# Second attention's score maxima as 32-row tiles in four banks, without head-separated keys

## The chip, the cores and the metric

The kernel runs on one core of a Trainium2 chip. The metric is the device time of one execution in microseconds (us). The engines are named as the profile names them: PE (TensorE matmuls), PEld (TensorE weight loads), DVE (VectorE), ACT (ScalarE), POOL (GpSimd) and SP (SyncE, which issues DMAs). PSUM, which the matmuls write, has eight banks of 512 float32 per partition.

## The reference

Two batches of 512 tokens with 128 features pass four sublayers, each after a layer norm and each added to its input: attention over a context of 154 keys (8 heads of 64), a feed-forward layer with 16 routed experts, attention over the same context (16 heads of 8), and a feed-forward layer with 8 routed experts.

```python
x = x + _L0_xattn_ref(_layernorm(x), ctx_768, ...)
x = x + _L0_ffn_ref(_layernorm(x), ...)
x = x + _L1_xattn_ref(_layernorm(x), ctx_768, ...)
x = x + _L1_ffn_ref(_layernorm(x), ...)
# the second attention, 16 heads of 8 features
scores = jnp.einsum('bhqd,bhkd->bhqk', q, k) * scale
weights = jax.nn.softmax(scores, axis=-1)
out = jnp.einsum('bhqk,bhkd->bhqd', weights, v)
```

## The kernel before

The work is cut into named steps: `h1` is one 128-wide hidden tile of a feed-forward layer for one batch, `down` the product back to 128 features, `score` and `pT` belong to the first attention. A table of strings, `PROGRAM`, writes out for each engine the order in which it takes its steps, and for PE also the PSUM bank behind each step (`score1.2` writes bank 2). Engines meet through two counters per bank: `wait_filled` waits until PE has filled a bank, `wait_moved` and `wait_bank_free` wait until a reader has emptied it. PE takes its steps strictly in the table's order, so a step whose bank is not free holds up all behind it.

The second attention of a batch b works on four groups g of four heads. In the features of a group, head j owns rows 32j to 32j+31 (its 8 features in several rounded parts, and two rows that carry the maximum). Its steps are, in order:

- `qd`, `q1` (PE, L1375): queries of all groups, four 32-row tiles at a time, one per group, copied to SBUF by ACT (`q1copy`, L828).
- `k1` (once for the kernel): the keys of a group, assembled by ACT (`rounded`) and DVE in `k_stack`. From this, `place_k1` on ACT (L817, 16 instructions) writes a tile `k1` in which each head's keys stand alone, with zeros in the other heads' rows, and `place_k1s` on POOL writes a like tile for the last 26 keys.
- `score1` (PE, L1384, 64 matmuls): scores for the maxima alone. All 128 rows of one group's queries for 128 tokens (t) are the stationary operand, and the head-separated keys of two heads, 308 columns, stream through. One matmul fills one bank.
- the same step on DVE (L1143, 64 reductions): the negated maxima of 2 heads by 128 tokens.
- `mT` (L1392): transposes the maxima of half h (two groups); ACT copies them and a DMA (`place_max`) writes them into rows of `q1`, after which `expT` (L1404) and `expR` (L1411) compute scores less maxima, transposed. ACT takes the exponentials (L845, L852).
- `rest1` and `pv1` (L1424, L1435), `od`, `oT`, `onT`, `wo1`: weighted values, division by the sums, output projection. Then the layer norm (`lnA`, `lnB`, `xT`), the router (`gate`, `route`), and the last feed-forward layer.

The lines of the step that changes:

```python
# PE, L1379 to L1385
b, t, g, half = step[1:]
wait_moved(pe, ("q1", b, g))
pe.wait_ge(k1_placed, 4 * (g + 1))
filled(pe.matmul(bank(step)[:, 0:2 * CTX]..., q1[:, b, g, t * P:(t + 1) * P],
                 k1[:, b, g, 2 * half:2 * half + 2, 0:CTX], start=True, stop=True), step)
# DVE, L1139 to L1145
wait_filled(dve, step)
moved(dve.tensor_reduce(neg_max1[:, b, g // 2, 2 * half:2 * half + 2, g % 2, t],
                        bank(step)[:, 0:2 * CTX]..., AX, ALU.max, negate=True), step)
```

Of the kernel before, what the change touches and what calls it, by code (L numbers as in the profile page):

```python
# [54 lines left out]
P = 128  # L55
B = 2
# [24 lines left out]
REST_SETS = ((0, 1), (2, 3))  # L81
LAST = (3, B - 1, N_HID[3] - 1)
# [4 lines left out]
def all_steps():  # L87
# [39 lines left out]
    steps += [("place_k1", g, j) for g in groups for j in range(4)]  # L127
# [49 lines left out]
    "ACT":  # L177
        "kT split lnB kT xT kT kT lnB q xT q split " + 16 * "score " +
        "pT score score pT k1 pT score pT score score split score pv pv score pv pv place_k1 score score " +
        "score score score split score score place_k1 pT score score place_k1 lnB pT k1 pT xT split k1 pT " +  # L180
# [24 lines left out]
        "hsplit h3 hsplit hsplit h3 res res res res last_res last_res ",  # L205
    "Pool":
        "lnA split lnA bo bo split " + 7 * "norm " + "lnA norm place_k1s split split split lnA place_k1s " +
        8 * "weigh " + "split split lnA " + 8 * "weigh " +
        "split split lnA split place_k1s place_k1s split split split lnA split split weigh weigh weigh weigh " +
        "weigh lnA " + 27 * "weigh ",  # L210
    "SP":
# [1327 lines left out]
```

## Time and profile before

| | |
|---|---|
| median of 3 runs (lowest to highest) | 231.21 us (231.13 to 231.42) |
| span of the profiled execution, first to last instruction | 229.8 us |
| median less that span | 1.4 us |
| PE busy | 223.2 us (97%), 1389 instructions |
| DVE / ACT / POOL busy | 163.5 / 155.3 / 126.4 us |
| TensorE clock granted | 1.00 of full speed in the whole span |

A busy time counts an instruction from its start to a modelled end, and matmuls overlap in the pipeline, so PE busy at 97% doesn't say that PE works at its best pace. The pace is read from starts: how long after one piece's first instruction the next piece's first instruction begins. A float32 matmul has two records in the trace, a matmul of rounded operands (fp32r) one. The profile gives no time of its own for the profiled execution besides the span; the 1.4 us between the span and the median are taken as lying around it.

### The profile page before, as it was taken

Reading aid. Unit: us, or ns where it says so; the run is one execution under the profiler, and the core shown is the slowest. Engines: PE = TensorE matmul, PEld = TensorE weight load, DVE = VectorE, ACT = ScalarE, POOL = GpSimd, SP = SyncE. Lnnn points to the kernel's source line nnn. Section 1 sums busy time; section 2 is a strip of 40 time slices with the busy share of each in tenths; the row PEclk is TensorE's granted clock in tenths of the full one; section 3 lists DMA queues with packets and bytes.
Section 4 is the critical chain, followed back from the end, with each engine's and each line's share of the span. In section 5 each row is a group of like instructions: output and inputs, shape, how many; then the busy total and the mean of one; then the engine's idle time right before and its main releaser. Section 6 shows DMA issues by size and latency. Waiting matters only on the chain.

```text
span 229.8 us, 4648 instructions
## 1 busy us (share of the span) xinstructions
PE 223.2 (97%) x1389; PEld 166.4 (72%) x1389; DVE 163.5 (71%) x480; ACT 155.3 (68%) x378; POOL 126.4 (55%) x127
## 2 busy tenths in 40 slices
PE   7999999999999999999999999999999999999994
PEld 3576765974989898889535563588878887888873
DVE  3689984788667953699948983564857776776874
ACT  2589999986678446662689788876365686645561
POOL 2766742898057927856592107209499400996540
PEclk9999999999999999999999999999999999999999
DMA  6890000000038924800600000037000003600002
GB/s 208 198 303 8 0 3 0 0 3 1 3 93 230 365 105 165 203 0 4 219 3 0 7 0 6 0 82 287 3 0 0 1 3 105 265 0 4 1 0 91
DMA packets 10174, 17.07 MB, mean 74 GB/s; under 512 B 3715, under 2 KB 5540, under 8 KB 9766
## 3 DMA queue, kind: packets, MB, share of 16 engines
q1 hardware_dynamic: 9926, 16.45, 23.1%
q10 hardware_dynamic: 224, 0.32, 0.4%
q8 instruction: 12, 0.20, 0.4%
q14 instruction: 12, 0.10, 0.1%
HBM read 16.08 MB, written 0.62 MB: 73 GB/s over the span
## 4 chain that ended last, share of the span: by engine, by line
PE 83%; ACT 6%; DVE 3%; DMA 2%; SPq 2%; POOL 2%; issue 1%; DVEq 0%; POOLq 0%
PE psum L1170 12%; PE psum L1173 11%; PE psum L1171 11%; PE psum L1326 7%; ACT prob L748 5%; PE psum L1384 5%; PE psum L1333 4%; PE psum L1335 3%; PE psum L1334 3%; PE psum L1435 3%; PE psum L1278 3%; PE psum L1288 3%; PE psum L1404 2%; PE psum L1256 2%; PE psum L1245 2%; DMA ctxT<-in_ctxT 2%
## 5 line engine op out<-in xcount | busy, mean ns | idle before, releaser
L702 POOL TENSOR_TENSOR act_s<-act_s,spread 128x512 f32<-128x512 f32 x35 | 44.4, 1292 | 19.8 <-DMA spread<-cw 13.6
L1170 PE MATMUL psum<-xT_hi,w_hi 128*128 128x512 f32 x108 | 43.9, 406 | 0.0
L1173 PE MATMUL psum<-xT_lo,w_hi 128*128 128x512 f32 x108 | 42.2, 391 | 0.0
L1171 PE MATMUL psum<-xT_hi,w_lo 128*128 128x512 f32 x108 | 42.2, 391 | 0.0
L797 ACT CAST q<-psum 128x512 fp32r<-128x512 f32 x35 | 20.4, 586 | 20.3 <-PE psum L1335 13.7
L1006 DVE TENSOR_TENSOR q<-psum,q 128x512 fp32r<-128x512 f32 x35 | 23.8, 687 | 13.3 <-ACT q L797 13.0
L787 ACT ACTIVATE act_s<-psum 128x512 f32<-128x512 f32 x39 | 23.0, 597 | 12.3 <-PE psum L1173 7.9
L1143 DVE TENSOR_REDUCE neg_max<-psum 128x2 f32<-128x308 f32 x64 | 26.2, 471 | 4.9 <-PE psum L1384 4.7
L702 POOL TENSOR_TENSOR hid<-hid,spread 128x512 f32<-128x512 f32 x13 | 16.6, 1297 | 18.9 <-DMA spread<-cw 14.6
L652 POOL TENSOR_TENSOR rstd<-vareps,minus_half 128x4 f32<-128x4 f32 x8 | 8.1, 1014 | 33.9 <-DVE vareps L907 33.9
L646 POOL TENSOR_TENSOR w_lo<-w_src,w_hi 128x768 fp32r<-128x768 f32 x12 | 21.7, 1830 | 8.9 <-ACT w_hi L717 8.9
L748 ACT ACTIVATE prob<-psum,neg_max 128x154 f32<-128x154 f32 x64 | 24.0, 405 | 1.7 <-DVE neg_max L949 1.0
L1170 PEld LDWEIGHTS psum<-xT_hi,w_hi 128*128 128x128 f32 x108 | 20.3, 188 | 5.5 <-ACT od L860 0.8
L1173 PEld LDWEIGHTS psum<-xT_lo,w_hi 128*128 128x128 f32 x108 | 20.3, 188 | 4.5
L676 POOL TENSOR_TENSOR prob_n<-prob,row_inv 128x1024 f32<-128x1024 f32 x8 | 15.2, 1899 | 13.9 <-DVE row_inv L956 13.9
L1171 PEld LDWEIGHTS psum<-xT_hi,w_lo 128*128 128x128 f32 x108 | 20.4, 188 | 3.3
L845 ACT ACTIVATE probT<-psum 128x512 f32<-128x512 f32 x32 | 16.8, 604 | 3.5 <-PE psum L1404 3.4
L1326 PEld LDWEIGHTS psum<-w,hid 128*128 128x128 f32 x144 | 17.5, 191 | 1.0 <-issue 0.4
L1326 PE MATMUL psum<-w,hid 128*128 128x128 f32 x144 | 18.1, 275 | 0.0
L1384 PE MATMUL psum<-k,q 128*128 128x308 f32 x64 | 16.0, 342 | 0.6 <-DVE neg_max L1143 0.5
L949 DVE TENSOR_REDUCE neg_max<-psum 128x2 f32<-128x308 f32 x32 | 13.5, 463 | 4.2 <-PE psum L1245 4.0
L1384 PEld LDWEIGHTS psum<-k,q 128*128 128x128 f32 x64 | 10.3, 188 | 8.1 <-DVE neg_max L1143 4.6
(171 smaller groups left out, 468.2 us busy)
## 6 DMA issues: line engine op xcount, KB each, us to landing
spread<-cw SPq DMA_DIRECT2D x16, 256.0 KB, 4.4
spread<-cw SPq DMA_DIRECT2D x6, 512.0 KB, 5.5
w_src<-in_w SPq DMA_DIRECT2D x2, 1152.0 KB, 5.3
w_src<-in_w SPq DMA_DIRECT2D x1, 2304.0 KB, 12.4
spread<-cw SPq DMA_DIRECT2D x8, 128.0 KB, 2.9
w<-in_w SPq DMA_DIRECT2D x1, 576.0 KB, 6.9
out<-X SPq DMA_DIRECT2D x4, 128.0 KB, 1.8
wv<-in_wv SPq DMA_DIRECT2D x2, 192.0 KB, 4.8
```

What stands on the lines that cost most here:

```text
L646: pool.tensor_tensor(lo, src, hi.bitcast(F32), ALU.subtract).then_inc(lo_of[name], 1)
L702: pool.tensor_tensor(g, g, spread[:, slot, :], ALU.mult).then_inc(weighed, 1)
L748: ins = act.activation(prob[:, r, h, 0:CTX], bank(step)[:, m * CTX:(m + 1) * CTX], ACT.Exp, bias=neg_max0[:, b, t, h:h + 1], accum_out=row ...
L787: moved(act.activation(act_buf(n), bank(step), ACT.Silu), step)
L797: act.copy(hid_hi[:, m % 2, :], bank(("h3",) + step[1:])).then_inc(hid_rounded, 1)
L1006: moved(dve.tensor_tensor(hid_lo[:, m % 2, :], bank(h3), hid_hi[:, m % 2, :].bitcast(F32), ALU.subtract), h3)
L1143: moved(dve.tensor_reduce(neg_max1[:, b, g // 2, 2 * half:2 * half + 2, g % 2, t], bank(step)[:, 0:2 * CTX].rearrange("p (j c) -> p j c", ...
L1170: pe.matmul(dst, w_hi, xT_hi[:, b, :], start=True, stop=False)
L1171: pe.matmul(dst, w_lo, xT_hi[:, b, :], start=False, stop=False)
L1173: return pe.matmul(dst, w_hi, xT_lo[:, b, :], start=False, stop=True)
L1326: ins = pe.matmul(bank(key)[:, t * P:(t + 1) * P], hid[:, n % HIDS, t * P:(t + 1) * P], w2_0[:, i, :], start=(i == 0 and t == 0), stop=las ...
L1384: filled(pe.matmul(bank(step)[:, 0:2 * CTX].rearrange("p (j c) -> p j c", j=2), q1[:, b, g, t * P:(t + 1) * P], k1[:, b, g, 2 * half:2 * h ...
```

## The change

- The four heads of a group are read in place. `k1` becomes the tile that DVE assembles (`k_stack` is gone), 16 `place_k1` instructions on ACT and the semaphore `k1_placed` go, and with them DVE's and PE's waits on it.
- `score1` becomes 12 steps (batch, half h, part c) in place of 64. A step covers three, three or two of the eight pairs (g, t) of a half (`PEAKS`). For each pair it issues four matmuls, one per head j, with 32 rows of queries as the stationary operand and 154 key columns, at the four row positions of the array, each into its own bank. So a step has 12 or 8 matmuls, takes four banks, waits for all four to be free before its first matmul, and signals each with its last. In all 128 matmuls stand for 64.
- `peak` is the reduction on DVE: one per bank, 3 x 154 = 462 elements (32 of them) or 308 (16), 48 in place of 64.
- `expT` reads the same keys from the new tile. All orders in `PROGRAM` are written anew, for every engine.

```diff
+PEAKS = ((0, 3), (3, 6), (6, 8))
...
-    steps += [("place_k1", g, j) for g in groups for j in range(4)]
-    steps += [("score1", b, t, g, half) for b in batches for h in range(2) for t in range(T) for g in REST_SETS[h] for half in range(2)]
+    steps += [("score1", b, h, c) for b in batches for h in range(2) for c in range(len(PEAKS))]
+    steps += [("peak", b, h, c, j) for b in batches for h in range(2) for c in range(len(PEAKS)) for j in range(4)]
...
-        "q1.1.6.0.4 pv1 score1.1 score1.7 expR.6 score1.2 expR.0 score1.1 score1.4 score1.7 expT.6.2 score1.1 " +
+        "score1.7.2.1.5 expR.4 expR.6 expT.7.4 pv1 expT.2.6 score1.1.5.7.4 rest1 pv1 score1.2.6.1.5 expT.7.4 " +
...
-                k1 = sb("k1", [P, B, G1, 4, CTX], F32R, r2)
+                k1 = sb("k1", [P, G1, B, CP], F32R, r2)
-                    k_stack = sb("k_stack", [P, 2, B * CP], F32R, r3)
...
-                    act.mul(k1[:, :, g, j, :], k[:, :, 0:CTX], head_rows[:, j:j + 1]).then_inc(k1_placed, 1)
...
+                    key = ("score1",) + step[1:]
+                    wait_filled(dve, key)
+                    moved(dve.tensor_reduce(neg_max1[:, b, h, j, lo:hi],
+                                            bank(key)[:, 0:(hi - lo) * CTX].rearrange("p (i c) -> p i c", i=hi - lo), AX, ALU.max,
+                                            negate=True), key)
...
+                    b, h, c = step[1:]
+                    keys = [step + (j,) for j in range(4)]
+                    for key in keys:
+                        wait_bank_free(pe, key)
+                    lo, hi = PEAKS[c]
+                    for n in range(lo, hi):
+                        g, t = REST_SETS[h][n // T], n % T
+                        wait_moved(pe, ("q1", b, g))
+                        wait_moved(pe, ("k1", g))
+                        for j, key in enumerate(keys):
+                            rows = slice(PAD * j, PAD * j + PAD)
+                            ins = pe.matmul(bank(key)[:, (n - lo) * CTX:(n - lo + 1) * CTX], q1[rows, b, g, t * P:(t + 1) * P],
+                                            k1[rows, g, b, 0:CTX], start=True, stop=True, skip_group_check=True,
+                                            tile_position=(PAD * j, 0))
+                            if n == hi - 1:
+                                filled(ins, key)
```

The second batch's part of the second attention on PE, from its queries (`q1`) on, stood so before; `q,k` of 128x308 is `score1`, `q,k` of 128x512 is `expT`, `probT,v` is `pv1`, `rest_exp,vs` is `rest1`:

```order
L1375 MATMUL psum<-qd,sel 128x512 x8
L1435 MATMUL psum<-probT,v 32x512 x4
L1384 MATMUL psum<-k,q 128x308 x2
L1411 MATMUL psum<-q,k1s 128x512
L1384 MATMUL psum<-k,q 128x308
L1411 MATMUL psum<-q,k1s 128x512
L1384 MATMUL psum<-k,q 128x308 x3
L1404 MATMUL psum<-q,k 128x512 x2
L1384 MATMUL psum<-k,q 128x308
L1404 MATMUL psum<-q,k 128x512 x2
L1384 MATMUL psum<-k,q 128x308 x3
L1424 MATMUL psum<-rest_exp,vs 32x512 x8
```

and stands so now, with `score1` at L1377 (128x154), `expT` at L1399, `expR` at L1406, `pv1` at L1430, `rest1` at L1419:

```order
L1360 MATMUL psum<-qd,sel 128x512 x8
L1430 MATMUL psum<-probT,v 32x512 x4
L1377 MATMUL psum<-k,q 128x154 x12
L1406 MATMUL psum<-q,k1s 128x512 x2
L1399 MATMUL psum<-q,k 128x512 x2
L1430 MATMUL psum<-probT,v 32x512 x4
L1399 MATMUL psum<-q,k 128x512 x2
L1377 MATMUL psum<-k,q 128x154 x12
L1419 MATMUL psum<-rest_exp,vs 32x512 x8
L1430 MATMUL psum<-probT,v 32x512 x4
L1377 MATMUL psum<-k,q 128x154 x8
L1399 MATMUL psum<-q,k 128x512 x2
```

Single score matmuls strewn between other steps have become blocks of 12 or 8. In `PROGRAM` the first three blocks take the banks 7 2 1 5, then 1 5 7 4, then 2 6 1 5; the two `expT` between the first and the second block take 7 4 and 2 6.

At the start of the program, PE stood so before; `wv,ctxT` of 128x512 is `vf`, the values of one batch for the first attention, 128x256 is `vf1`, `ident,xn` is `xT`:

```order
L1186 MATMUL psum<-ctxT,wk 128x320 x4
L1226 MATMUL psum<-ident,xn 128x128 x4
L1202 MATMUL psum<-wv,ctxT 128x512
L1202 MATMUL psum<-wv,ctxT 128x256
L1170 MATMUL psum<-xT_hi,wq_hi 128x512
```

and stands so now:

```order
L1171 MATMUL psum<-ctxT,wk 128x320 x4
L1187 MATMUL psum<-wv,ctxT 128x512
L1211 MATMUL psum<-ident,xn 128x128 x4
L1187 MATMUL psum<-wv,ctxT 128x512
L1187 MATMUL psum<-wv,ctxT 128x256
L1155 MATMUL psum<-xT_hi,wq_hi 128x512
```

The second batch's `vf` now comes before the first query product; before, it stood behind the seventh `scores` step. At the end of the first attention two hidden tiles of the next layer (`h3.2 h1.0`) now stand ahead of the last `pT` steps, where before they came after the values.

## Rows read from the trace of the kernel before

**Rows 1.** The page's head: span, busy time and instructions of each engine.

```profile
span 229.8 us, 4648 instructions
PE 223.2 (97%) x1389; PEld 166.4 (72%) x1389; DVE 163.5 (71%) x480; ACT 155.3 (68%) x378; POOL 126.4 (55%) x127
```

**Rows 2.** Busy time by stretch: us, PE, PEld, DVE, ACT, POOL, clock, DMA share, GB/s.

```profile
13.80:52.90 39.10, 38.09 (x353) 28.61 (x352) 31.93 (x81) 35.49 (x154) 24.70 (x24) 1.00 0.09 25
...
109.30:120.30 11.00, 10.41 (x70) 4.61 (x69) 7.68 (x24) 8.18 (x17) 8.26 (x11) 1.00 0.35 116
120.30:136.30 16.00, 15.81 (x104) 9.50 (x100) 14.45 (x40) 12.93 (x25) 2.47 (x2) 1.00 0.01 3
...
150.00:224.00 74.00, 74.00 (x340) 60.70 (x339) 51.78 (x112) 45.01 (x82) 42.49 (x36) 1.00 0.17 58
```

**Rows 3.** Timeline of PE, 16 to 51 us: start, busy us, what [idle before, releaser].

```profile
16.80 0.79 PE L1245 MATMUL psum<-k,q 64*128 64x154 f32 x8 [0.38 <-ACT prob L748]
17.54 1.12 PE L1202 MATMUL psum<-wv,ctxT 96*128 96x512 f32 x2
18.28 0.62 PE L1170 MATMUL psum<-xT_hi,wq_hi 128*128 128x512 f32 x1
...
50.92 1.28 PE L1256 MATMUL psum<-ident,prob_n 128*128 128x128 f32 x10 [0.53 <-POOL prob_n L679]
```

**Rows 4.** Timelines of ACT and DVE, 8 to 11 us: the first query product's operands.

```profile
8.76 0.58 ACT L728 CAST xT_hi<-psum 128x512 fp32r<-128x512 f32 x1 [0.27 <-PE psum L1226]
...
9.94 0.68 DVE L912 TENSOR_TENSOR xT_lo<-psum,xT_hi 128x512 fp32r<-128x512 f32 x1
```

**Rows 5.** Timeline of PE, 95 to 99 us, and PEld's row of the first step.

```profile
95.57 0.30 PEld L1375 LDWEIGHTS psum<-qd,sel 32*128 32x128 f32 x8
...
95.57 0.74 PE L1375 MATMUL psum<-qd,sel 32*128 32x512 f32 x8
96.24 1.16 PE L1326 MATMUL psum<-w,hid 128*128 128x128 f32 x8
...
98.22 0.87 PE L1384 MATMUL psum<-k,q 128*128 128x308 f32 x5
98.92 0.39 PE L1170 MATMUL psum<-xT_hi,w_hi 128*128 128x512 f32 x1
```

**Rows 6.** Timeline of PE: one and three `scores` steps of the first attention.

```profile
22.43 0.79 PE L1245 MATMUL psum<-k,q 64*128 64x154 f32 x8
23.16 0.66 PE L1256 MATMUL psum<-ident,prob_n 128*128 128x128 f32 x4
...
37.41 1.84 PE L1245 MATMUL psum<-k,q 64*128 64x154 f32 x24
```

**Rows 7.** Timeline of PE, 109 to 110 us: `expT`, then `score1`.

```profile
109.31 0.49 PE L1404 MATMUL psum<-q,k 32*128 32x512 f32 x2
109.74 0.55 PE L1384 MATMUL psum<-k,q 128*128 128x308 f32 x2
```

**Rows 8.** Timeline of PE, 52 us: two of the router's sixteen narrow matmuls.

```profile
52.18 0.26 PE L1300 MATMUL psum<-gates_parts,xT_hi 128*128 128x32 f32 x1
52.29 0.26 PE L1301 MATMUL psum<-gates_parts,xT_lo 128*128 128x32 f32 x1
```

**Rows 9.** Timeline of DVE: reductions, and two products of 512 elements.

```profile
105.59 1.27 DVE L1108 TENSOR_TENSOR hid<-psum,act_s 128x512 f32<-128x512 f32 x2
...
120.72 2.79 DVE L1143 TENSOR_REDUCE neg_max<-psum 128x2 f32<-128x308 f32 x7 [2.46 <-PE psum L1384]
...
135.65 0.48 DVE L1143 TENSOR_REDUCE neg_max<-psum 128x2 f32<-128x308 f32 x1 [0.23 <-PE psum L1384]
```

**Rows 10.** Timeline of ACT, 119 to 122 us; and `place_k1` among the groups by line.

```profile
119.35 2.05 ACT L828 CAST q<-psum 128x512 fp32r<-128x512 f32 x4 [0.66 <-PE psum L1375]
121.26 1.13 ACT L852 ACTIVATE rest_exp<-psum 128x512 f32<-128x512 f32 x2
...
L817 ACT ACTIVATE k<-k_stack,head_rows 128x308 fp32r<-128x308 f32 x16 | 8.1, 547 | 0.0
```

More of the change, by code:

```diff
@@ L206 @@
-    "Pool":
[L207 to L210, printed above, removed]
[20 rows of a table added]
+    "ACT":
+        "split kT kT lnB kT xT lnB split kT q q xT score score score score score score score score score score " +
+        "score score score score score score pT score score score score pT pT score pT k1 score split pv score " +
+        "pv pv pv score score split score score score score pT score score score lnB pT k1 xT pT h1 pT gate k1 " +
+        "k1 pv pv split pv pv h1 cwT h1 h1 h1 lnB xT gate h1 h1 split h1 h1 h1 cwT h1 h1 h1 h1 lnB split xT qd " +
+        "h1 h1 split q1copy q1copy q1copy q1copy split h1 split h1 split mT exp exp exp exp expR exp lnB expR xT " +
+        "exp exp qd mT exp q1copy q1copy q1copy q1copy expR expR exp exp exp exp od exp exp exp exp mT od split " +
+        "expR exp exp onT expR exp mT exp exp exp exp exp expR lnB expR xT exp exp exp exp exp exp exp route exp " +
+        "h1 cwT split h1 hsplit od h1 h1 od h1 hsplit h1 h1 hsplit onT hsplit h1 hsplit h1 split hsplit hsplit " +
+        "h1 h1 hsplit h1 h1 hsplit h1 hsplit lnB hsplit split h1 xT hsplit h1 hsplit hsplit h1 route hsplit h1 " +
+        "h1 hsplit h1 h1 cwT hsplit h1 h1 h1 h1 hsplit hsplit hsplit ycopy hsplit h1 h1 hsplit hsplit hsplit h1 " +
+        "h1 hsplit ycopy hsplit h1 h1 h1 hsplit h1 h1 hsplit hsplit h1 hsplit hsplit hsplit hsplit h1 hsplit " +
+        "hsplit ycopy ycopy ",
@@ L211 @@
     "SP":
-        "store spread spread spread spread spread fetch store spread spread spread spread spread place_max " +
-        "fetch place_max place_max place_max store spread spread spread spread spread store spread spread " +
-        "spread spread spread out out out out ",
+        "store spread spread spread spread spread fetch store spread spread spread spread spread place_max fetch " +
+        "place_max place_max place_max store spread spread spread spread spread store spread spread spread " +
@@ L215 @@
+        "spread spread out out out out ",
 }
@@ L221, in takes @@
     if engine == "PE":
-        return True
-    if kind in ("scores", "q1", "expT"):
+        return kind != "peak"
+    if kind in ("scores", "q1", "expT", "score1"):
         return False
@@ L260, in bank_uses @@
             keys = [step[:3] + (2 * step[3] + j,) for j in range(2)]
+        elif kind == "score1":
+            keys = [step + (j,) for j in range(4)]
         elif kind == "pv1":
@@ L421, in build @@
         k1_rounded = sem("k1_rounded")
-        k1_placed = sem("k1_placed")
         sel_built = sem("sel_built")
@@ L810, in _ @@
                     act.copy(rounded[:, g % 2, 0:B * CP], bank(step)[:, 0:B * CP]).then_inc(k1_rounded, 1)
-                elif kind == "place_k1":
-                    g, j = step[1:]
-                    wait_moved(act, ("k1", g))
-                    act.wait_ge(loaded["const"], 16 * N_CONST)
-                    k = k_stack[:, g % 2, :].bitcast(F32).rearrange("p (b c) -> p b c", b=B)
-                    act.mul(k1[:, :, g, j, :], k[:, :, 0:CTX], head_rows[:, j:j + 1]).then_inc(k1_placed, 1)
                 elif kind == "qd":
@@ L857, in _ @@
                         wait_filled(act, ("oT", 0, k))
-                    act.wait_ge(k1_placed, 4 * G1)
-                    act.wait_ge(k1s_placed, G1)
+                    wait_moved(act, ("k1", G1 - 1))
                     moved(act.copy(od[:, k, :], bank(("pv1", b, k))), ("pv1", b, k))
@@ L1115, in _ @@
                     dve.wait_ge(loaded["const"], 16 * N_CONST)
-                    if g >= 2:
-                        dve.wait_ge(k1_placed, 4 * (g - 1))
-                        dve.wait_ge(k1s_placed, g - 1)
-                    moved(dve.scalar_tensor_tensor(k_stack[:, g % 2, :], rounded[:, g % 2, 0:B * CP].bitcast(F32), lo_rows[:, 1:2],
+                    moved(dve.scalar_tensor_tensor(k1[:, g, :, :].rearrange("p b c -> p (b c)"), rounded[:, g % 2, 0:B * CP].bitcast(F32), lo_rows[:, 1:2],
                                                    bank(step)[:, 0:B * CP], ALU.mult, ALU.add), step)
@@ L1138, in _ @@
                     moved(dve.tensor_tensor(qd[:, 1, :], bank(step), qd[:, 0, :].bitcast(F32), ALU.subtract), step)
-                elif kind == "score1":
-                    b, t, g, half = step[1:]
-                    wait_filled(dve, step)
-                    moved(dve.tensor_reduce(neg_max1[:, b, g // 2, 2 * half:2 * half + 2, g % 2, t],
-                                            bank(step)[:, 0:2 * CTX].rearrange("p (j c) -> p j c", j=2), AX, ALU.max, negate=True),
-                          step)
+                elif kind == "peak":
+                    b, h, c, j = step[1:]
+                    lo, hi = PEAKS[c]
[4 more added lines that the diff above has]
+                                            negate=True), key)
                 elif kind == "oT":
@@ L1379, in _ @@
                 elif kind == "score1":
-                    b, t, g, half = step[1:]
-                    wait_moved(pe, ("q1", b, g))
-                    pe.wait_ge(k1_placed, 4 * (g + 1))
-                    filled(pe.matmul(bank(step)[:, 0:2 * CTX].rearrange("p (j c) -> p j c", j=2), q1[:, b, g, t * P:(t + 1) * P],
-                                     k1[:, b, g, 2 * half:2 * half + 2, 0:CTX], start=True, stop=True), step)
+                    b, h, c = step[1:]
+                    keys = [step + (j,) for j in range(4)]
+                    for key in keys:
+                        wait_bank_free(pe, key)
+                    lo, hi = PEAKS[c]
+                    for n in range(lo, hi):
[9 more added lines that the diff above has]
+                                filled(ins, key)
                 elif kind == "mT":
                     b, h = step[1:]
-                    for g in REST_SETS[h]:
-                        for half in range(2):
-                            wait_moved(pe, ("score1", b, T - 1, g, half))
-                    filled(pe.transpose(bank(step)[0:PAD, 0:P], neg_max1[:, b, h, :, :, :].rearrange("p j g t -> p (j g t)"),
+                    for j in range(4):
+                        wait_moved(pe, ("score1", b, h, len(PEAKS) - 1, j))
+                    filled(pe.transpose(bank(step)[0:PAD, 0:P], neg_max1[:, b, h, :, :].rearrange("p j n -> p (j n)"),
                                         ident[:, :]), step)
@@ L1403, in _ @@
                         rows = slice(PAD * j, PAD * j + PAD)
-                        filled(pe.matmul(bank(key), k1[rows, b, g, j, 0:P], q1[rows, b, g, :], start=True, stop=True,
+                        filled(pe.matmul(bank(key), k1[rows, g, b, 0:P], q1[rows, b, g, :], start=True, stop=True,
                                          skip_group_check=True, tile_position=(PAD * j, 0)), key)
```

45 lines of the change are left out of this document (19 added, 26 removed), and 45 rows, old and new, of the table PROGRAM.

## Prediction

> **What bounds the kernel now.** I read the page's head first, then the table by stretch, then timelines of PE, DVE and ACT by start times. The head gives PE 223.2 of 229.8 us, 97%; the other engines stay under 72% [rows 1]. The reader is to see that PE is the engine to count, and also that a busy 97% says little about pace, as ends are modelled. The table by stretch tells four places apart [rows 2]. From 150 to 224 us PE is busy 74.00 of 74.00: the last feed-forward layer streams, and the change does not touch it but for the order of its steps. From 13.8 to 52.9, the first attention, PE is busy 38.09 of 39.10 and ACT 35.49: PE leads, ACT is close. From 109.3 to 120.3 PE idles 0.59 us. From 120.3 to 136.3, the second batch's maxima, DVE is busy 14.45 of 16.00: there I take DVE as the bound and PE as filled up with what fits between. So one thing removed from PE is worth its price in the first and in the feed-forward stretches, and little in the last.
>
> **Prices.** Prices are start to start. A `score1` took 0.70/5 = 0.14 us, from 98.22 to 98.92 [rows 5]. A pair of `expT` took 0.43 [rows 7] for two 512-column streams side by side, at `score1`'s pace 0.14 x 512/308 = 0.23; the 0.2 left over is the change between 32-row tiles and the whole array, which I take as **0.2 us for a change of mode**. Counted in the program, PE has 70 such changes before and 78 after, since six blocks per batch stand between other kinds of step. The new round (four matmuls of 32 rows and 154 columns, in one row position each) is in no row. From below, a stream of 154 columns at `score1`'s pace is 0.14 x 154/308 = 0.07. From above, `scores`, two row tiles of 64 with 154 float32 columns: 24 against 8 matmuls took (1.84 - 0.79)/2 = 0.525 more per eight [rows 6], so four rounds of two, 0.131 each, with two passes each; four row tiles at that rate, if only two pairs ran side by side, would be 0.262. Nearest is a matmul bound by its weight load: the router's narrow ones follow each other at 0.11 us with 32 columns [rows 8], and each matmul of a new round loads 128 columns too. Loads one after the other, 0.44, are excluded: eight loads of `q1` lay in 0.30 and its block took 0.67 [rows 5]. I take **0.111 us a round**, with 0.07 and 0.262 as ends.
>
> The Trainium skill (TensorE: Matmul & The Clock Gate, Part 3, The mechanism) says that a weight load overlaps running matmuls only where its row group differs. By that the four loads of a round run side by side, but each waits for its own row's stream of the round before: rival B below. The `scores` rows speak against it, at 0.131 a round for two passes with nothing added for loads.
>
> **Part one, the first attention.** `vf` of the second batch took 17.54 to 18.28, 0.74 us [rows 3]. It goes to the start, ahead of `xT`. There it delays `xT_hi`, which ended at 9.34, while `xT_lo` began on DVE only at 9.94 [rows 4], 0.6 later; and DVE's order, too, has the two layer norms before it. So up to 0.74 comes back (the lower end is nothing); I take 0.74 - 0.6 and about a change of mode, 0.3, hence -0.45. PE's idle 0.38 for ACT at 16.80 [rows 3] is from a modelled end; by the pace of `scores` (0.79 shown for 0.525, [rows 6]) it is 0.38 + 0.27 = 0.65. The moved order has other products there, and it goes: -0.65. The idle 0.53 for POOL's `prob_n` at 50.92 [rows 3] is likewise 0.7 by pace, and `h3`, `h1` now stand there: -0.7. Two changes of mode more: +0.4. On ACT 16 `place_k1` of 0.547 us go, 8.8 us [rows 10]; three lie inside this stretch, 1.6 us, so ACT (35.49 of 39.10) does not become the bound in its place. The others lie beside FFN work of PE and give nothing. Together **-1.4**; bounds -2.1 and 0.
>
> **Part two, from the first batch's queries to the last `down` before 109.3.** 22 `score1` at 0.14 are 3.1 us. In their place stand 11 rounds at 0.111, 1.2 us, and 8 changes of mode at 0.2, 1.6 us: 2.8. **-0.3**; with the round at 0.07 -0.75, at 0.262 +1.3.
>
> **Part three, the chain of the second batch's maxima.** (a) PE's idle 0.59 in 109.3 to 120.3 [rows 2] is a wait for banks that DVE is late to empty; with fewer reductions still due there, the queries come some 0.55 earlier. (b) Reductions: one of 308 takes (2.79 - 0.48)/6 = 0.386 from start to start, with 135.65's 0.48 as a lone one [rows 9]. One of 462 I place by the product of 512 elements, 1.27 for two, 0.6 each [rows 9]: between the two 0.548. 16 x 0.548 + 8 x 0.386 = 11.86 against 32 x 0.386 = 12.35: -0.5. If a reduction were all fixed cost, 24 x 0.386 would be 9.3, -3.1; at 0.6 for 462 it would be +0.3. (c) The waits. Before, a bank freed was refilled one by one, and DVE stood idle in this chain some 1.0 us (16.00 less 14.45, less 0.5 at the ends [rows 2, 9]). Now a block waits for all four of its banks. The second block has banks 4 and 7 behind the first four exponentials. On ACT these stand behind four `q1copy`, 2.05 us, and two `expR`, 1.13 [rows 10]. I count 1.0 for that boundary, 0.35 for the next, where PE has `rest1` and `pv1` between, and nothing for three: 1.35, or +0.35. ACT's freeing of those banks is the cover; where it is later, this rises. (a), (b) and (c): **-0.7**; bounds -3.3 and +2.6 (the rival F).
>
> **Part four, behind the chain.** Two pairs of `expT` that stood before the gate now stand behind it, where FFN1's hidden tiles wait: 0.43 [rows 7] and one change of mode, 0.2: **+0.65**.
>
> DVE drops 16 reductions and waits for `k1_placed`; PE too. SP's order is the same, POOL's steps are the same in another order, and no DMA is added or gone. **Sum: -1.4 - 0.3 - 0.7 + 0.65 = -1.75 us.** The profiled execution has 229.8 us of span and 1.4 around it, 231.2, which is the median of the runs (231.21). 231.2 - 1.75 = **229.5 us**. A difference under 0.2%, 0.46 us, is no difference that a measurement can tell.
>
> **Rivals.** *B, loads not hidden:* a round costs 0.111 + 0.07 = 0.18; 11 rounds of the first batch and as many of the second are on PE's path: 22 x 0.07 = +1.5, **231.0**, no change. For it: a round has the same four row positions as the one before. Against: the `scores` rows. *G, the first attention gives nothing,* as ACT paces it (35.49 of 39.10): +1.4, **230.9**. Against: the two idles are there in PE's rows. *C, narrow streams cost two passes:* 0.262 a round, 22 x 0.15 = +3.3, **232.8, slower.** Place: every block; decides from 0.19 us a round (1.75/22 + 0.111). For it: `scores`, also 154 columns, also row tiles. Against: `scores` has float32 operands, and `score1` rounded ones, which before ran 308 columns in 0.14. *F, DVE starves at the block boundaries:* at each of the five, DVE must empty the last bank before PE may begin: a change of mode 0.2, the block 0.33, and 0.31 (a `score1`'s own length, 0.87 - 4 x 0.14 [rows 5]) make 0.85; 5 x 0.85 = 4.25 instead of 1.35: +2.9, **232.4, slower.** For it: banks recur from block to block (5, 1, 7 or 4). Against: each block has at least one new bank, and `expT`, `pv1`, `rest1` lie between. *E, all of PE's saving arrives:* 64 x 0.14 - 32 x 0.111 = 5.4, less six further changes of mode, 1.2, is 4.2; with the first attention's 1.4, **225.6.** Against: DVE's 14.45 of 16.00 [rows 2].
>
> The Trainium skill (TensorEngine Tiling, PSUM Bottleneck) says that packing speeds up PE but not the emptying of PSUM, which may become the bound. That is F's side against E; the table's 14.45 of 16.00 for DVE agrees.
>
> **How the numbers follow.** Forecast 0.44 (its own range 228.4 to 230.7: the round between 0.07 and 0.16, the start between 0 and 0.74); B 0.08, G 0.08, C 0.18, F 0.12, E 0.10. 227.5 to 233.0 leaves out most of E and the tail of C and F with another stretch lost, under 0.2. Faster by over 0.2% is below 230.75: 0.42 of the forecast, all of E, 0.04 of G and 0.02 of B: 0.58. Slower, above 231.7: C, F and 0.02 of the forecast: 0.32. Within: 0.10.
>
> **What would show it.** Start to start, a block of 12 matmuls should take 0.33 us, and 0.2 for the mode; 0.54 is B, 0.79 is C. PE's idles at `scores` for ACT and at `pT` for POOL should be gone. The second batch's peaks, 15.4 us from first start to last end before [rows 9], should take about 15.2, with one idle of 1 us on DVE; five of 0.85 are F. FFN1's first product should come some 1.7 us earlier. Wrong it would be if a peak of 462 elements takes far from 0.55 us, or if a step in the first attention waits anew.

## The result, and the profile after

The changed kernel takes 234.94 us (median of 4 runs, 234.25 to 236.79) beside 231.31 for the kernel before on the same chip (231.13 to 231.86): a ratio of 1.0152, 95% interval 1.0118 to 1.0186. The forecast was 229.5 with a range up to 233.0. The profiled execution has a span of 235.0 us, and 236.79 as its own time, the longest of the four. Ratios, here and below, leave out executions that lie over 1.5% above the fastest of the same kernel.

The page, busy tenths of PE and the granted clock in 40 slices of 5.9 us:

```profile
PE   7999899999999999999799889999999999999994
...
PEclk9999999999999999999879967999999999999999
```

In the kernel before, the clock's row is nines from end to end. Now it dips twice, in the second attention. By stretch, in the two windows that were shown of before [rows 2] and one behind them (columns as in [rows 2]):

```profile
109.30:120.30 11.00, 9.69 (x72) 5.08 (x74) 8.71 (x24) 7.53 (x16) 7.16 (x9) 0.81 0.31 115
120.30:136.30 16.00, 13.04 (x138) 5.53 (x130) 11.49 (x27) 11.21 (x21) 0.00 (x0) 0.95 0.01 3
136.30:145.00 8.70, 8.70 (x54) 4.37 (x54) 4.68 (x18) 4.47 (x9) 1.81 (x4) 0.60 0.02 5
```

PE, busy 15.81 of 16.00 us in the maxima's stretch before, is now busy 13.04. DVE, which I took to bind there, shows 11.49 instead of 14.45, but most of that is the chain of the maxima coming 2.1 us later: over the chain itself, below, DVE is busy 13.72 of 15.72 us, before 14.45 of 15.41. Cut at the dips:

```profile
112.00:116.00 4.00, 2.81 (x29) 1.62 (x27) 3.93 (x16) 3.70 (x9) 3.17 (x7) 0.95 0.74 295
116.10:119.50 3.40, 3.35 (x22) 1.26 (x22) 1.93 (x4) 2.59 (x6) 1.19 (x1) 0.50 0.00 0
133.00:136.60 3.60, 2.16 (x27) 1.45 (x27) 3.57 (x10) 2.89 (x5) 0.00 (x0) 0.95 0.02 5
136.65:143.50 6.85, 6.85 (x40) 3.64 (x36) 4.33 (x17) 4.01 (x9) 0.49 (x1) 0.50 0.02 6
```

Twice the clock stands at 0.50 (1.2 in place of 2.4 GHz), 10.2 us in all, and ahead of both PE is busy for only 2.81 of 4.00 and 2.16 of 3.60 us. (In this execution the clock reads 0.95 elsewhere; in a second profile of the same kernel, below, it reads 1.00 there, and the halved stretches come in the same two passages.) PE's timeline has the idles:

```profile
101.31 0.57 PE L1377 MATMUL psum<-k,q 32*128 32x154 f32 x12
101.81 0.50 PE L1155 MATMUL psum<-xT_hi,w_hi 128*128 128x512 f32 x1
...
104.86 0.47 PE L1377 MATMUL psum<-k,q 32*128 32x154 f32 x8
105.26 2.06 PE L1311 MATMUL psum<-w,hid 128*128 128x128 f32 x16
...
114.66 0.47 PE L1377 MATMUL psum<-k,q 32*128 32x154 f32 x8 [0.76 <-ACT probT L833]
...
119.99 0.74 PE L1360 MATMUL psum<-qd,sel 32*128 32x512 f32 x8
...
122.22 0.59 PE L1377 MATMUL psum<-k,q 32*128 32x154 f32 x12 [0.47 <-ACT q L816]
...
131.05 0.69 PE L1377 MATMUL psum<-k,q 32*128 32x154 f32 x12 [0.49 <-DVE neg_max L1128]
...
136.26 0.47 PE L1377 MATMUL psum<-k,q 32*128 32x154 f32 x8 [1.14 <-DVE on L1144]
...
138.85 2.08 PE L1455 MATMUL psum<-wo,onT 128*128 128x128 f32 x8
140.72 0.42 PE L1387 MATMUL psum<-ident,neg_max 128*32 128x128 f32 x1
```

The first four rows give the two prices that I had to choose: a block of 12 takes 0.50 us from start to start and one of 8 takes 0.40, so a round is 0.10 and the change of mode 0.20. The rows with brackets are blocks that waited for one of their four banks. The last two show the output projection at half clock: its 8 matmuls take 1.87 us from start to start, which before stood as two fours of 0.59 and 0.62. DVE's peaks of the second batch:

```profile
122.82 2.27 DVE L1128 TENSOR_REDUCE neg_max<-psum 128x3 f32<-128x462 f32 x4 [3.15 <-PE psum L1377]
126.56 2.28 DVE L1128 TENSOR_REDUCE neg_max<-psum 128x3 f32<-128x462 f32 x4 [1.47 <-PE psum L1377]
129.05 1.64 DVE L1128 TENSOR_REDUCE neg_max<-psum 128x2 f32<-128x308 f32 x4 [0.21 <-PE psum L1377]
...
131.73 3.37 DVE L1128 TENSOR_REDUCE neg_max<-psum 128x3 f32<-128x462 f32 x6 [0.24 <-PE psum L1377]
...
135.82 2.72 DVE L1128 TENSOR_REDUCE neg_max<-psum 128x3 f32<-128x462 f32 x6
```

The chain takes 122.82 to 138.54, 15.7 us, where it took 15.4 [rows 9]. It has one long idle, 1.47 at the first boundary (forecast 1.0). The first peak comes 2.83 us after the queries' first matmul (119.99), where before it came 2.11 after (118.61 and 120.72). So neither the round's price nor a DVE that starves makes the loss. The chain itself is 0.3 longer, its start 0.7 later, and much of the rest is the clock.

### The profile page after: what moved, and what is told of

Same layout as the page of the kernel before. It is cut to its first block and busy times, and to the rows that moved or that the text cites. A ratio compares the mean times of both kernels' runs of the same rounds, so it can differ in the third digit from the quotient of the medians.

```text
span 235.0 us, 4720 instructions
## 1 busy us (share of the span) xinstructions
PE 224.9 (96%) x1453; PEld 164.1 (70%) x1453; DVE 162.7 (69%) x464; ACT 150.5 (64%) x364; POOL 126.3 (54%) x127
## 5 line engine op out<-in xcount | busy, mean ns | idle before, releaser
L993 DVE TENSOR_TENSOR q<-psum,q 128x512 fp32r<-128x512 f32 x35 | 23.9, 689 | 15.3 <-ACT q L792 14.8
L1128 DVE TENSOR_REDUCE neg_max<-psum 128x3 f32<-128x462 f32 (+1 forms) x48 | 24.9, 578 | 6.7 <-PE psum L1377 6.7
L671 POOL TENSOR_TENSOR prob_n<-prob,row_inv 128x1024 f32<-128x1024 f32 x8 | 15.2, 1898 | 13.6 <-DVE row_inv L943 13.6
L833 ACT ACTIVATE probT<-psum 128x512 f32<-128x512 f32 x32 | 17.3, 601 | 2.8 <-PE psum L1399 2.7
L1311 PE MATMUL psum<-w,hid 128*128 128x128 f32 x144 | 18.7, 280 | 0.0
L936 DVE TENSOR_REDUCE neg_max<-psum 128x2 f32<-128x308 f32 x32 | 13.9, 467 | 5.0 <-PE psum L1230 5.0
L1095 DVE TENSOR_TENSOR hid<-psum,act_s 128x512 f32<-128x512 f32 x18 | 12.2, 686 | 6.5 <-POOL act_s L697 5.0
L1097 DVE TENSOR_TENSOR psum<-psum,act_s 128x512 f32<-128x512 f32 x20 | 13.8, 693 | 3.1 <-PE psum L1158 1.7
```

Of the source, the lines that this page charges most:

```text
L833: moved(act.activation(probT1[:, n % 2, j, :], bank(("expT",) + step[1:]), ACT.Exp, scale=HEAD_SCALE1), ("expT",) + step[1:])
L993: moved(dve.tensor_tensor(hid_lo[:, m % 2, :], bank(h3), hid_hi[:, m % 2, :].bitcast(F32), ALU.subtract), h3)
L1128: moved(dve.tensor_reduce(neg_max1[:, b, h, j, lo:hi], bank(key)[:, 0:(hi - lo) * CTX].rearrange("p (i c) -> p i c", i=hi - lo), AX, ALU.m ...
L1311: ins = pe.matmul(bank(key)[:, t * P:(t + 1) * P], hid[:, n % HIDS, t * P:(t + 1) * P], w2_0[:, i, :], start=(i == 0 and t == 0), stop=las ...
```

## The experiments

The theory after the result ("clock theory" below): **the blocks' waits leave PE idle, the clock falls to half behind them, and that costs 3 to 4 us.** Rivals: the waits alone; the new orders of the first attention and the first feed-forward layer; the tiles' waits for four banks at once, whatever the clock does. A first run of the changed kernel by itself:

> The changed kernel itself once more, for a profile to read the others against. In the first profile of it the granted clock never read above 0.95, and two stretches, 116.1 to 119.5 and 136.7 to 143.5 us, read 0.50. Clock theory: the two halved stretches come back at the same places, each behind an idle of PE of 0.7 to 1.2 us at a score block, and the span is near 233. Rival (the halved stretches were that execution's chance): no stretch at 0.50, span near 230.

It took 237.44 us, with 0.50 in two stretches of 6.83 us each, 114.6 to 121.4 and 138.5 to 145.3 us of its span, and 1.00 elsewhere. The drops are the kernel's: every run of it that was timed had a mean granted clock below 1 (0.931 to 0.983). The kernel before isn't quite free of them: four of its executions beside these runs read 0.991 to 0.993, and took 232.73 to 233.32 us.

### Fillers: the clock by itself

Fillers, matmuls whose results nobody reads, were put where PE waits, into a bank of the waiting step as soon as that one is free; the step overwrites them.

```diff
+FILL = {("score1", 0, 1, 2): (1, 3), ("score1", 1, 0, 0): (0, 3), ("expT", 1, 0, 0): (0, 2), ("score1", 1, 1, 0): (0, 2),
+        ("score1", 1, 1, 2): (0, 5)}
...
+                    j, n = FILL[step]
+                    wait_bank_free(pe, keys[j])
+                    rows = slice(PAD * j, PAD * j + PAD)
+                    for _ in range(n):
+                        pe.matmul(bank(keys[j]), sel[rows, 0, :, :, :].rearrange("p j s d -> p (j s d)"),
+                                  k1[rows, 0:2, :, :].rearrange("p g b c -> p (g b c)")[:, 0:512], start=True, stop=True,
+                                  skip_group_check=True, tile_position=(PAD * j, 0))
```

> PE's five longest idles at score blocks and expT of the second attention are filled with 15 matmuls of 32 rows by 512 columns, whose results are overwritten. Clock theory: no stretch, or a much shorter one, at 0.50; 10.2 us at half clock cost about 4 us (1.3 in the first stretch, 2.7 in the second), so 231 us. Rival, the waits alone (four banks at once hold PE and DVE up, and the clock only goes with it): nothing of the waits is gone, so the time stays at 234.5 to 235.3.

Measured: 1.0121 (1.008 to 1.0162), clock 0.978 to 0.992; its eight executions lie between 232.97 and 237.05 us. The waits are filled, yet in the profiled execution the clock falls at the same two places. The whole-array form differs in two lines:

```diff
-                    rows = slice(PAD * j, PAD * j + PAD)
+                    rows = slice(0, P)
...
-                                  skip_group_check=True, tile_position=(PAD * j, 0))
+                                  skip_group_check=True)
```

> As the one with 32-row fillers, but the 15 matmuls use all 128 rows, at the price of two changes of mode at each of the five places. Clock theory: 231 to 232 us, the clock 1.00 or nearly so. Waits alone: 235 to 236, the fillers' changes of mode on top. If the clock asks for work of the whole array, this one gains and the 32-row one doesn't.

Measured: 1.0069 (1.0042 to 1.0095), clock 0.998 to 1.00 in all eight runs; once more on another chip:

> The filled kernel with full-array fillers again, as the partner of the three that follow on the same chip. Clock theory: clock 1.00, ratio to before between 1.004 and 1.010, as at first.

1.0049 (1.003 to 1.0067). The two fillers set side by side, by stretch, first the 32-row one (two places where the clock falls, and what stands ahead of each), then the whole-array one:

```profile
112.40:115.40 3.00, 2.86 (x20) 1.63 (x18) 2.99 (x7) 2.82 (x7) 2.82 (x5) 1.00 0.62 252
115.45:118.85 3.40, 3.26 (x21) 1.11 (x20) 1.77 (x3) 2.21 (x5) 0.75 (x1) 0.50 0.00 0
132.90:135.90 3.00, 3.00 (x22) 2.37 (x22) 2.97 (x9) 2.22 (x4) 0.00 (x0) 1.00 0.00 0
135.92:142.74 6.82, 6.82 (x37) 3.64 (x36) 4.20 (x17) 3.97 (x9) 0.46 (x1) 0.50 0.02 6
```

```profile
112.40:115.40 3.00, 2.80 (x20) 1.69 (x20) 3.00 (x7) 2.79 (x7) 2.70 (x5) 1.00 0.75 301
132.90:135.90 3.00, 3.00 (x20) 1.78 (x20) 2.67 (x8) 1.70 (x4) 0.00 (x0) 1.00 0.00 0
```

PE reads busy 2.86 and 3.00 of 3.00 ahead of the falls, and 2.80 and 3.00 where the clock stays. So in these two kernels a full busy row doesn't tell whether the clock stays; with whole-array matmuls in those places it stayed in all 14 executions, with 32-row ones in none of eight. The times go with it: from the first `expT` to the second batch's queries and from the last peak to the last layer's first product, the 32-row one takes 9.33 and 11.43 us, the whole-array one 8.25 and 8.82. Within one kernel, too: the one with its waits taken ahead, below, took 231.58 to 233.50 us in eight executions at 0.999 to 1.00, 234.29 in one at 0.993 and 234.89 in one at 0.983. So the clock does cost this time. Its rival, the waits alone, would have left the whole-array one at 1.015 or above.

What makes the clock fall is less clear. The idles alone don't account for it: it fell where they were filled with 32-row matmuls. The score matmuls themselves are now 32-row ones in place of whole-array ones, and no run separates that from the blocks' waits.

What remains over the kernel before was partly the fillers' own. In the five-place kernel the three ahead of the second batch's first block end about 0.7 us after the banks it waits for are free. Three kernels have fewer places; the first of them, the lean one, has three:

```diff
-FILL = {("score1", 0, 1, 2): (1, 3), ("score1", 1, 0, 0): (0, 3), ("expT", 1, 0, 0): (0, 2), ("score1", 1, 1, 0): (0, 2),
-        ("score1", 1, 1, 2): (0, 5)}
+FILL = {("score1", 0, 1, 2): (1, 3), ("score1", 1, 1, 0): (0, 2), ("score1", 1, 1, 2): (0, 3)}
```

> Full-array fillers at three places only, 3, 2 and 3 of them. In the five-place kernel the three ahead of the second batch's first block ended 0.7 us after the queries' banks could have been ready, and the five ahead of the last block about 0.3 us late. Clock theory with overshoot: clock 1.00 and 0.7 to 1.0 us under the five-place kernel, ratio 1.001 to 1.003. If the idle ahead of the first block drops the clock by itself: a halved stretch near 120, and no gain.

Measured: 1.0016 (0.999 to 1.0043), clock 0.993 to 1.00, 1.00 in ten of twelve runs. The other two have one entry each, `("score1", 0, 1, 2): (1, 3)` and `("score1", 1, 1, 2): (0, 5)`:

> Fillers only at the idle near 114 us, ahead of the first batch's last block. If each halved stretch has its own idle: the one at 116 is gone and the one at 137 stays, time 1.0 to 1.5 us under the changed kernel, ratio 1.008 to 1.011. If the clock falls for the whole passage: both stay, or the first only moves, ratio 1.015.

> Fillers only at the idle near 135 us, ahead of the second batch's last block. If each halved stretch has its own idle: the one at 137 is gone, the one at 116 stays, time 2 to 2.5 us under the changed kernel, ratio 1.005 to 1.008. Otherwise a stretch of 0.50 still follows the second batch's blocks, ratio 1.012 to 1.015.

Measured: 1.0097 (1.0065 to 1.013) and 1.0143 (1.011 to 1.0175). Their rows of the clock:

```profile
PEclk9999999999999999999997979999999999999999
```

```profile
PEclk9999999999999999999859899999999999999999
```

With the first idle filled, the first dip is gone from its place and a short one comes later, at 123 us, the other staying at 137. With the last filled, the first dip stays and another lies at 132 us, ahead of the filler. So an idle doesn't own a dip, which I had expected. Of the kernels run, those with whole-array fillers in one place lose the clock in every execution; with three or five places most executions hold it, but not all: the five-place kernel with slowed blocks, below, read 0.978 to 0.985 in four executions of six.

### The first attention and its order

Old front: all orders ahead of the first batch's queries as before the change (without `place_k1`), banks renumbered to fit, the rest as changed. In `PROGRAM`, the first line for PE, as the last of these four kernels has it:

```diff
-        "kT.0 kT.1 kT.2 kT.3 vf.4 xT.5 vf.6 vf1.7 q.0 q.1 q.2 q.5 xT.4 scores.7.3 scores.0.1 scores.2.5 vs.6 q.4 " +
+        "kT.0 kT.7 kT.0 kT.6 xT.5 vf.7 vf1.4 q.6 q.5 q.4 xT.6 q.5 scores.4.0 scores.5.7 scores.6.3 " +
...
```

> The new tiles and all orders from the second attention's first queries on as changed; all orders ahead of that as before the change, without the 16 place_k1. Orders theory (the new order of the first attention and first feed-forward layer loses what my part one expected to win): the first batch's q1 starts 1 to 1.5 us earlier and the time falls to 233.5. Clock theory: the loss lies behind q1, so the time stays within 0.5 us of 234.9. My prediction's part one: 1.4 us slower, 236.3.

> As the kernel with the old front, but with the front's banks renumbered, so that the first hidden tile behind it doesn't wait for the bank of the queries (that wait cost 1.4 us there), and POOL's old order kept through the first feed-forward layer. Front theory (the new front gains about 0.5 us up to the router, and its feed-forward layer gives back 1.2): 0.3 to 0.8 us faster than the changed kernel, ratio to before 1.012. My prediction's part one: 1.4 us slower than it, 1.021.

> The mended old front and the 15 full-array fillers together. Clock theory: clock 1.00 and about 0.8% under the unfilled one. If front theory holds too: ratio 1.003 to 1.005, 0.3 to 0.8 us under the filled kernel with the new front.

> The old front again, with the banks renumbered a second time: in the earlier two with the old front PE idled 1.4 and 1.7 us ahead of the queries for banks that DVE was still emptying, at the seam that I made. If the new front wins what my part one expected (1.4 us): ratio 1.013, as with that idle. If it wins 0.6 up to the router and the feed-forward layer gives 1.1 back: 1.003 to 1.006, 0 to 0.8 us under its partner.

Measured: 1.0226 (1.0183 to 1.0269), 1.0222 (1.0199 to 1.0246), 1.0135 (1.0108 to 1.0162) and 1.0105 (1.0078 to 1.0132). Read by these alone, the new front would win 0.6%, as my part one had it. But each of the four has an idle at the seam that I made between old orders and new, ahead of the first batch's queries or the tile before them, 1.4, 1.4, 1.7 and 1.1 us; in the two filled ones:

```profile
96.38 0.74 PE L1375 MATMUL psum<-qd,sel 32*128 32x512 f32 x8 [1.69 <-DVE hid L1100]
```

```profile
96.07 0.74 PE L1375 MATMUL psum<-qd,sel 32*128 32x512 f32 x8 [1.07 <-ACT act_s L787]
```

Its partner is the kernel with the same fillers and the new front. Less that idle the last one stands at 1.0105 - 1.07/231.7 = 1.006 beside 1.0049 for its partner, and the third at 1.0135 - 1.69/231.6 = 1.006 beside 1.0069. That is worked out, not run: no kernel with the old front and without the idle was made. By it the new front with the feed-forward layer behind it wins nothing that shows. The traces say where. From the second profile of the changed kernel:

```profile
11.25 0.47 PE L1158 MATMUL psum<-xT_lo,wq_hi 128*128 128x512 f32 x1
...
26.07 0.80 PE L1230 MATMUL psum<-k,q 64*128 64x154 f32 x8 [0.72 <-issue]
...
52.86 0.26 PE L1285 MATMUL psum<-gates_parts,xT_hi 128*128 128x32 f32 x1
...
95.28 0.74 PE L1360 MATMUL psum<-qd,sel 32*128 32x512 f32 x8
```

and from the kernel before, the same product and the first of the router's matmuls:

```profile
10.78 0.41 PE L1173 MATMUL psum<-xT_lo,wq_hi 128*128 128x512 f32 x1
...
51.96 0.26 PE L1300 MATMUL psum<-gates_parts,xT_hi 128*128 128x32 f32 x1
```

Both idles of before are gone, for ACT and for POOL [rows 3]. But PE now waits 0.72 ahead of a `scores` at 26.07, and 0.66 to 0.77 there in every profile with the new front. The trace names no releaser; ACT works without a break from 21.63 to 26.26 us, so it may be ACT again. From that first product to the router it is 41.2 us before and 52.86 - 11.25 = 41.6 after, of which 1.4 are the two hidden tiles moved ahead: a gain of 0.9, and 0.74 of it is the moved `vf`. Then the feed-forward layer up to the queries: 43.6 us before; after, it holds one hidden tile (0.68) and two `down` (1.78) less, so 41.1 were due, and the profiled executions with the new front show 41.8 to 42.6. So 0.7 to 1.4 are given back there; what by is not shown (the second profile names one wait of 0.20 us).

### Whole blocks or bank by bank

In the second batch, the matmuls of one bank in a row, each bank waited for by itself:

```diff
+                    order = [(n, j) for n in range(lo, hi) for j in range(4)]
+                    if b == 1:
+                        order.sort(key=lambda nj: nj[1])
...
+                    for n, j in order:
...
+                        if b == 1 and n == lo:
+                            wait_bank_free(pe, key)
+                        wait_moved(pe, ("q1", b, g))
+                        wait_moved(pe, ("k1", g))
```

> The changed kernel, but the second batch's six blocks run bank by bank (two or three matmuls of one row position in a row) and wait for each bank on its own. Block theory (waiting for four banks at once delays the second batch's first peak by 0.7 to 1.2 us against its queries and makes PE idle): first peak 2.1 to 2.5 us behind the queries in place of 2.8 to 3.3, PE's idles before blocks shorter, and 0.7 us off the time; more, up to 2.5, if the second halved stretch of the clock goes. Clock theory alone: idles of a like length stay at the last bank, time and clock as in the changed kernel. Price: a block of three per bank takes 0.07 x 9 to 0.1 x 12 = 0.6 to 1.2 us.

> Bank by bank and the full-array fillers together. Clock theory and block theory both right: ratio about 1.003, 0.7 us under the filled kernel with whole blocks (1.0069). If only the clock counts: 1.007.

Measured: 1.0286 (1.0262 to 1.031) and 1.0241 (1.0201 to 1.0281), clock 0.976 to 0.986 and 0.978 to 0.998. Neither theory had this, and it is already there in the first batch, where the order of the matmuls is the changed kernel's and only the two waits ahead of each are new:

```profile
101.42 1.12 PE L1382 MATMUL psum<-k,q 32*128 32x154 f32 x12
102.47 0.50 PE L1155 MATMUL psum<-xT_hi,w_hi 128*128 128x512 f32 x1
```

The block takes 1.05 in place of 0.50. These two kernels tell nothing of the blocks, but something of waits. Two kernels with the waits taken ahead of the block, one bank by bank (there each bank's own wait stays ahead of its matmuls), one in whole blocks:

```diff
+                    groups_in = sorted({REST_SETS[h][n // T] for n in range(lo, hi)})
...
+                    for g in groups_in:
+                        wait_moved(pe, ("q1", b, g))
+                        if b == 0:
+                            wait_moved(pe, ("k1", g))
```

> Bank by bank again, with only the wait for its bank ahead of each bank's matmuls. The earlier one had two waits before every matmul, which were long met, and its blocks of 12 took 1.0 to 1.1 us in the first batch where only those waits were added, against 0.50. Block theory: first peak of the second batch at most 2.5 us behind the queries in place of 3.2, 0.5 to 0.8 us under its partner. If matmuls of one row position in a row can't overlap their loads (0.1 a matmul), a block takes 1.2 us: same time as its partner or up to 1 us slower.

> As its partner, with each block's waits for queries and keys ahead of its first matmul and without repeats. If a met wait costs PE 0.03 us, as the first bank-by-bank kernel suggests, blocks of 12 take 0.40 in place of 0.50 and those of 8 0.35, and where PE leads (the first batch's first four blocks) 0.3 to 0.4 us is won; the rest hides. If it costs nothing between matmuls: block 0.50, time as its partner.

Measured: 1.0063 (1.0036 to 1.0089) and 1.0049 (1.0021 to 1.0077) beside 1.0049 for the partner: nothing that shows is won or lost by either. Each lost the clock in some executions, two of ten (0.985 and 0.993) and three of eleven (0.983 to 0.993). A block run bank by bank takes what a whole one takes, 0.52 from start to start:

```profile
120.53 0.59 PE L1399 MATMUL psum<-k,q 32*128 32x154 f32 x12
121.05 0.74 PE L1429 MATMUL psum<-q,k1s 128*128 128x512 f32 x2
```

Its first peak still came 3.17 us behind the queries, as the fillers kept PE until 120.53; so the theory that the wait for four banks at once is what delays the peaks is not settled by it. What the lean kernel, which has no filler there, shows is that the block starts when its second bank of queries has been copied (0.50 of waiting for ACT), and the first peak then comes 2.83 us behind the queries, 0.7 later than before:

```profile
119.73 0.60 PE L1389 MATMUL psum<-k,q 32*128 32x154 f32 x12 [0.50 <-ACT q L817]
120.26 0.73 PE L1419 MATMUL psum<-q,k1s 128*128 128x512 f32 x2
```

### The kernel before, with less work on PE

This "thin" kernel leaves out half of the second batch's scores for the maxima.

```diff
-                    filled(pe.matmul(bank(step)[:, 0:2 * CTX].rearrange("p (j c) -> p j c", j=2), q1[:, b, g, t * P:(t + 1) * P],
-                                     k1[:, b, g, 2 * half:2 * half + 2, 0:CTX], start=True, stop=True), step)
+                    some = 1 if b == 1 else 2
+                    filled(pe.matmul(bank(step)[:, 0:some * CTX].rearrange("p (j c) -> p j c", j=some), q1[:, b, g, t * P:(t + 1) * P],
+                                     k1[:, b, g, 2 * half:2 * half + some, 0:CTX], start=True, stop=True), step)
```

> The kernel before, with the second batch's scores for the maxima of one head in place of two per matmul (154 of 308 columns; the other head's maxima come from what the bank held). PE has 32 x 0.07 = 2.2 us less to do in a stretch that DVE bounds; everything else waits as before. If less work there is enough to lose the clock: a stretch of 0.50 in or behind 120 to 137 us, and 1 to 3 us slower. If it takes long waits: clock 1.00, time within 0.3% of before.

Measured: 0.997 (0.9949 to 0.9991), clock 0.991 to 1.00, as the kernel before shows it too. Less work on PE alone doesn't lose the clock there. With single matmuls strewn between other steps, some 2.2 us less of PE (an estimate, 32 matmuls at half of 0.14) even shorten the chain that I took as bound by DVE: it goes from 120.75 to 135.55, 14.8 us for 15.4.

## Why the prediction was wrong

Two things together. The step that failed with the larger price: **in part three I priced the new waits for what they hold up, DVE's peaks, and took PE's own idles there as free.** Nothing in the sum says that the clock could change, and all its prices are at 1.00. The rows of before were at hand: from 120.3 to 136.3 PE was busy 15.81 of 16.00 us [rows 2], and I wrote that work taken from PE there was worth little. Less work there is harmless by itself, as the thin kernel shows. What I didn't see is that in blocks the room becomes idles at their starts: over the chain PE is busy 13.23 of 15.72 us, before 15.22 of 15.41, and the clock falls to half. The other fall lies in the stretch ahead of it, where part three had PE's idle vanish; it grew from 0.59 [rows 2] to 1.31 of 11.00 us. The Trainium skill (TensorE: Matmul & The Clock Gate, A second HAM failure mode: psum-queue depth-cycling) describes a kernel whose PE idles briefly between groups of matmuls as it cycles through banks, with the clock going back and forth. The rows here agree, idles of 0.5 to 1.1 us and two falls, though the falls stayed when 32-row matmuls filled them. It speaks against such a change, and I did not weigh it.

What the clock costs: the changed kernel less the lean one, 1.0152 - 1.0016 = 1.4%, 3.1 us. By rows, first of the changed kernel, then of the lean one:

```profile
110.73 0.50 PE L1399 MATMUL psum<-q,k 32*128 32x512 f32 x2
...
149.85 0.50 PE L1155 MATMUL psum<-xT_hi,w_hi 128*128 128x512 f32 x1
```

```profile
109.32 0.50 PE L1412 MATMUL psum<-q,k 32*128 32x512 f32 x2
...
117.49 0.74 PE L1371 MATMUL psum<-qd,sel 32*128 32x512 f32 x8
118.16 1.07 PE L1443 MATMUL psum<-probT,v 128*32 128x512 f32 x8
...
133.28 2.71 DVE L1129 TENSOR_REDUCE neg_max<-psum 128x3 f32<-128x462 f32 x6
...
144.65 0.50 PE L1156 MATMUL psum<-xT_hi,w_hi 128*128 128x512 f32 x1
```

From the first `expT` (110.73) to the queries (119.99) 9.26 us where the lean one takes 8.17 (109.32 to 117.49), and from the last peak's end (138.54) to the last layer's first product (149.85) 11.31 where the lean one takes 8.66 (135.99 to 144.65). That is 3.7 together, of which the base reading of 0.95 in that execution has some.

The second: with the clock held, the sum should have come out at -1.75, and what comes out is 1.0016, no change. Point by point, at full clock:

- **Prices of the round and of the mode:** right. 0.10 for 0.111, and 0.20 for 0.2. Rivals B (0.18) and C (0.262) fall.
- **Part one, -1.4:** half right, and given back. Up to the router -0.9 for the -1.7 due from the first product on: the idle for POOL went, and where the one for ACT went, 0.72 came back at another `scores`. What failed is the sentence that it "goes". The start can't be judged: the first product's third matmul lies between 10.3 and 11.8 us in the executions, whatever the order. And the term for the feed-forward layer is missing altogether: I read its order as moved work only, and it gives 0.7 to 1.4 back. G, that the first attention gives nothing, is about what was left; whether by its reason, ACT's pace, is not shown.
- **Part two, -0.3:** nearly right. 13.74 us before, 2 `down` more (1.78) and a hidden tile less (0.68) in it after, so 14.84; measured 14.8 to 15.1, about nothing.
- **Part three, (a) -0.55:** wrong in kind. The idle didn't go, it grew to 1.31. With the clock held it takes 8.1 to 8.3 us from `expT` to the queries for 9.3, but these -1.1 are one `pv1` of 1.11 us, which the new order takes from ahead of the queries to behind them, and for which the sum has no term. In the lean kernel's timeline none stands between `expT` and queries; in the kernel before the two stood so:

```profile
117.50 1.06 PE L1435 MATMUL psum<-probT,v 128*32 128x512 f32 x8
118.61 0.73 PE L1375 MATMUL psum<-qd,sel 32*128 32x512 f32 x8
119.28 1.06 PE L1435 MATMUL psum<-probT,v 128*32 128x512 f32 x8
```

- **(b) the reductions:** right. 462 elements take (3.37 - 2.28)/2 = 0.545, forecast 0.548.
- **(c) the waits:** the first boundary 1.47 for 1.0, the others together 0.45 for 0.35, so F falls. The moved `pv1` stands at the first boundary (124.45 to 125.47), so some of the 1.47 may be its price; no run separates it. And the block ahead of all boundaries was not in the count. It takes two of the queries' own banks, so it starts behind two copies by ACT and ends 12 matmuls later: +0.7. The chain is 15.7 where 15.2 was due.
- **Part four, +0.65:** wrong the other way. At full clock the part behind the chain takes 8.66 for 8.90, so nothing was lost there.

Summed in the order of the kernel (first attention, feed-forward layer, part two, the moved `pv1`, the first peak's delay, the chain, part four), -0.9 + 1.0 + 0 - 1.1 + 0.7 + 0.3 - 0.2 = -0.2 us, which fits the lean kernel's 1.0016 (0.999 to 1.0043). E, that all of PE's saving arrives, falls; but the thin kernel before shows that my reason against it, a stretch bound by DVE, was too simple.

None of the versions of the changed kernel beats the kernel before by more than can be told; the lean fillers bring it level.

## What to carry to other kernels

Work that is taken from PE where other engines set the pace turns into idles, and strewn single matmuls that look like filler may be what holds the clock; so when a change gathers them into blocks that wait for several banks, look at the granted clock first, and price the stretch behind each block at half clock as a rival. A hybrid of two written-out orders makes waits of its own at the seam: read the idle there before believing its time. In a change of order, each wait that "goes" needs the place named where its engine is late next, and before a shorter stretch is put down to a wait, its steps are to be counted: one may have moved out of it.

## What the runs showed that I had not expected

- The clock fell to half behind idles of at most 1.2 us, and with 32-row matmuls in them it fell even where PE read busy 3.00 of 3.00 us; with 15 whole-array matmuls in the same places it stayed at 0.998 to 1.00.
- Two waits that are long met, ahead of each matmul of a block, more than doubled it (1.05 for 0.50 us, some 0.06 for each of the nine matmuls that had none before), while waits ahead of every fourth one cost nothing that shows (0.50 with them and with all waits ahead of the block).
- The order of the matmuls over the four row positions made no difference to a block of 12: 0.52 us bank by bank, 0.50 to 0.53 in rounds.
